# Loads, copies and small operations moved around the stage boundaries of a cross-attention and feed-forward kernel

## The reference

```python
x = x + xattn(layernorm(x), ctx)          # 4 batches of 512 rows, D = 1024, 64 context rows each
x = x + ffn(layernorm(x))
# xattn: q, k, v by Wq, Wk, Wv (16 heads of 96, 4 kv heads), softmax(q k / sqrt(96)) v, times Wo
# ffn:
rw = sum(top_k(z @ gate_w, 2))            # z = layernorm(x)
h = relu(z @ up_w) ** 2
y = h @ down_w + ((z @ fc1_w) @ expert_w * rw) @ fc2_w
x = x + ((y - mean(y)) * rsqrt(var(y) + 1e-5) * gamma + beta)
```

## Time and profile before

| | |
|---|---|
| median of three runs | 2058.83 us (2056.39 to 2061.26) |
| the profiled execution: its time, its span | 2057.5 us, 2055.7 us |
| TensorE busy, weight loads busy | 1988.4 us (97%), 1652.6 us (80%) |
| VectorE, ScalarE, GpSimd busy | 1206.9 (59%), 796.4 (39%), 798.2 us (39%) |
| mean granted TensorE clock | 0.985 |
| DMA moved | 357.83 MB, mean 174 GB/s |
| stage C, D, E on TensorE, from about | 917, 1237.8, 1654 us |

### The profile page before, as it was taken

How to read it: one execution, slowest core, us unless ns; L and a number is a source line. 1 busy time by engine, 2 the same in 40 slices (tenths; PEclk the granted TensorE clock), 3 DMA queues, 4 the chain that set the end, 5 groups by cost and what they waited for, 6 DMA issues and landing times. The chain is left out here.

```text
span 2055.7 us, 28449 instructions
## 1 busy us (share of the span) xinstructions
PE 1988.4 (97%) x9068; PEld 1652.6 (80%) x9068; DVE 1206.9 (59%) x1689; ACT 796.4 (39%) x1246; POOL 798.2 (39%) x593
## 2 busy tenths in 40 slices
PE   8999999999999999999899888999999999999996
PEld 7888888888888888887788676787778878888885
DVE  4222212178888888851334249987976754445698
ACT  5121111157777777761111115322634434333221
POOL 2533030137777777673112212111111155445442
PEclk9999999999999999999999999999999999999998
DMA  6754332536556666535577883657454576675755
GB/s 196 253 173 152 134 143 93 172 91 148 145 151 163 154 146 150 144 105 154 180 199 218 237 217 116 215 180 199 165 175 162 192 242 200 218 230 161 243 176 170
DMA packets 352573, 357.83 MB, mean 174 GB/s; under 512 B 148064, under 2 KB 246368, under 8 KB 351584
## 3 DMA queue, kind: packets, MB, share of 16 engines
q1 hardware_dynamic: 269856, 301.46, 47.2%
q10 hardware_dynamic: 82624, 55.19, 11.0%
HBM read 231.51 MB, written 124.80 MB: 173 GB/s over the span
## 5 line engine op out<-in xcount | busy, mean ns | idle before, releaser
L139 PE MATMUL psum<-operands 128*128 128x512 f32 (+3 forms) x2728 | 1058.6, 388 | 48.6 <-POOL operands L1507 14.1
L140 PE MATMUL psum<-operands 128*128 128x512 f32 (+3 forms) x2728 | 1055.2, 387 | 0.0
L141 PE MATMUL psum<-operands 128*128 128x512 f32 (+3 forms) x2728 | 1052.2, 386 | 0.0
L139 PEld LDWEIGHTS psum<-operands 128*128 128x128 f32 (+1 forms) x2728 | 518.1, 190 | 148.0 <-issue 35.5
L141 PEld LDWEIGHTS psum<-operands 128*128 128x128 f32 (+1 forms) x2728 | 518.3, 190 | 101.1
L140 PEld LDWEIGHTS psum<-operands 128*128 128x128 f32 (+1 forms) x2728 | 519.0, 190 | 89.1
L2378 POOL TENSOR_TENSOR operands<-operands 128x640 fp32r<-128x640 f32 x112 | 198.0, 1781 | 204.4 <-ACT operands L2374 204.3
L1183 DVE TENSOR_REDUCE small<-psum 128x1 fp32r<-128x576 f32 x256 | 192.9, 754 | 90.0 <-PE psum L1009 89.9
L926 POOL TENSOR_TENSOR operands<-staging,operands 128x512 fp32r<-128x512 f32 x128 | 164.4, 1292 | 30.5 <-ACT operands L1103 21.7
L1877 POOL TENSOR_TENSOR operands<-plain,operands 128x1024 fp32r<-128x1024 f32 x17 | 50.0, 2940 | 305.7 <-ACT operands L1869 305.7
L2374 ACT ACTIVATE operands<-operands 128x640 fp32r<-128x640 f32 x112 | 80.8, 735 | 200.7 <-DMA operands<-h_operand_scratch 200.7
(11 more groups left out here) (148 smaller groups left out, 1807.5 us busy)
## 6 DMA issues: line engine op xcount, KB each, us to landing
h_operand_scratch<-staging SPq DMA_DIRECT2D x70, 512.0 KB, 3.1
operands<-h_operand_scratch SPq DMA_DIRECT2D x112, 320.0 KB, 4.3
plain<-in_down_w SPq DMA_DIRECT2D x29, 512.0 KB, 6.3
plain<-in_up_w SPq DMA_DIRECT2D x28, 512.0 KB, 5.8
operands<-recip_scratch SPq DMA_DIRECT2D x64, 192.0 KB, 4.2
o_scratch<-staging SPq DMA_DIRECT2D x64, 192.0 KB, 5.0
operands<-o_scratch SPq DMA_DIRECT2D x64, 192.0 KB, 4.5
operands<-q_hi_scratch ACTq DMA_DIRECT2D x14, 768.0 KB, 6.0
```

The source lines that it names most:

```text
L139: e.matmul(o, lh, rh, start=first, stop=False)
L140: e.matmul(o, lh, rl, start=False, stop=False)
L141: return e.matmul(o, ll, rh, start=False, stop=last)
```

## The change

- **SP in stage C**: unit 0 of tile n + 1 is loaded right behind the store of x1 of tile n - 1, units 1 and 2 behind the load of the x row, the stores of x1 + beta and the fold, and unit 3 behind D's first loads; before, all four stood behind all of these. Expert_w and the first fc2_w quarter are loaded one tile sooner, each further quarter too.
- **ScalarE at the end of C**: z_hi 1, w_hi 1, w_hi 5, z_hi 6 and z_hi 5 stand ahead of the last z_out of the tiles, w_hi 6 behind it.
- **The turned z of jobs 4 and 5** goes to the staging (`SF[:, 6 D: 10 D]`), not to the place where z_sum 6 is written; the wait for their stores moves from `z_sum` to `u_sums(0)`.
- **VectorE**: w_lo 5 behind z_lo 5 at D's start; in the second half z_sum 5 behind `u_sums`, z_sum 4 and z_lo 6 ahead of `h21`. ScalarE's z_hi 5 of the second half is one step earlier.
- **Stage E**: units 6 and 7 are loaded ahead of the next pass's weights; the three small norm operations run on ScalarE behind the root; the last tile's last operation and its store are made in two halves, one stored by SP and one by ScalarE.

```diff
 def z_turned(j):
-    to = (plain((4 if j < 4 else 36) * D, SLOT), plain((6 if j < 4 else 38) * D, SLOT))[j % 2] if j < Z_EARLY else SF[:, 2 * D:3 * D]
+    if j < 4:
+        to = (plain(4 * D, SLOT), plain(6 * D, SLOT))[j % 2]
+    elif j < Z_EARLY:
+        to = SF[:, (6 + 2 * (j % 2)) * D:(8 + 2 * (j % 2)) * D]
+    else:
+        to = SF[:, 2 * D:3 * D]
     return to.rearrange("p (t d) -> p t d", d=D)
...
     def tiles(b, t0):
-        if b == FB:
-            e.dma_start(ex_raw, expert_w).then_inc(f_xld, 16)
-        for r in range(2 * G):
-            e.wait_ge(*past(b_os[r], b * (H // (2 * G) * 16) + H // (2 * G) * 16))
-            e.sem_inc(idle, 1)
         for t in range(t0, ST):
             n = b * ST + t
-            for u in range(0 if n != 1 else 3, 4):
-                c_load_unit(e, b, t, u)
             e.wait_ge(*past(cc_x1, n))
...
             e.dma_start(x1_d[bass.ds(n * P - P, P), :], XR).then_inc(cc_st, 16)
+            if n == FB * ST - 1:
+                e.dma_start(ex_raw, expert_w).then_inc(f_xld, 16)
+                f_load(e, 0)
+            if b == FB and t + 1 < NQ:
+                f_load(e, t + 1)
+            if n < LAST_C:
+                next_units(n + 1, (0,))
             e.wait_ge(*past(cc_st, n * 16))
...
                 e.dma_start(xb_tiles(n)[0], beta.partition_broadcast(P)).then_inc(bet_l, 16)
-            if b == FB:
-                f_load(e, t)
-                if t:
-                    f_store(e, t - 1)
+            if b == FB and t:
+                f_store(e, t - 1)
             if b == FB + 1 and t == 0:
                 f_store(e, NQ - 1)
+            if n < LAST_C:
+                next_units(n + 1, (1, 2))
             d_first_loads(e, n)
+            if n < LAST_C:
+                next_units(n + 1, (3,))
+    def next_units(n, units):
+        b, t = n // ST, n % ST
+        if t == 0 and 0 in units:
+            for r in range(2 * G):
+                e.wait_ge(*past(b_os[r], b * (H // (2 * G) * 16) + H // (2 * G) * 16))
+                e.sem_inc(idle, 1)
+        for u in units:
+            c_load_unit(e, b, t, u)
+    c_load_unit(e, 0, 1, 3)
     tiles(0, 1)
...
             f_evac(e, NQ - 1)
+        if n == LAST_C:
+            z_hi(e, 0, 1)
+            w_hi_op(e, 0, 1)
+            w_hi_op(e, 0, 5)
+            z_hi(e, 0, 6)
+            z_hi(e, 0, 5)
         if n >= 5 and n % 2 == 1:
             z_out(e, (n - 5) // 2)
-    z_hi(e, 0, 1)
-    w_hi_op(e, 0, 1)
-    w_hi_op(e, 0, 5)
+    w_hi_op(e, 0, 6)
...
     w_sum_op(e, 0, 6)
-    w_lo_op(e, 0, 5)
     w_sum_op(e, 0, 7)
...
     z_lo(e, 0, 5)
+    w_lo_op(e, 0, 5)
     tile(LAST_C)
...
         e.wait_ge(*past(z_tn, sum(Z_TURNS[:Z_EARLY])))
-    if q == 0 and p == 6:
-        z_stored(e, Z_EARLY - 2)
-        z_stored(e, Z_EARLY - 1)
     if p == 5:
...
-    z_hi(e, 0, 5)
-    z_hi(e, 0, 6)
-    w_hi_op(e, 0, 6)
     z_hi(e, 0, 2)
...
             z_hi(e, 1, 6)
+            z_hi(e, 1, 5)
         if end:
...
         if it == NF5 - 1:
-            z_hi(e, 1, 5)
             z_hi(e, 1, 7)
...
             e.wait_ge(*past(cc_st, 16 * B * ST))
+            z_stored(e, Z_EARLY - 2)
+            z_stored(e, Z_EARLY - 1)
         e.tensor_tensor(O22, product_bank(it, 6), O11, ALU.add).then_inc(d_sm, 1)
...
         prepare, end = it + 1 in FIRST_STEP, it == NIT - 1
+        if it == NF5:
+            z_sum(e, 1, 4)
+            z_lo(e, 1, 6)
         if it:
...
         if it == NF5:
-            z_sum(e, 1, 4)
-            z_lo(e, 1, 6)
             z_lo(e, 1, 2)
...
             w_sum_op(e, g + 1, 5)
+        u_sums(it)
         if it == NF5 - 1:
             z_sum(e, 1, 5)
-        u_sums(it)
         if it == 0:
...
 SUMS_A = [2, 1, 0, 1, 0, 0, 0]
-E_CHAIN, E_ROOT = 9, 4
+E_CHAIN, E_ROOT = 6, 5
...
         s, pr = g // NPR, g % NPR
+        if g == 0:
+            e_unit_load(e, NU)
+            e_unit_load(e, NU + 1)
         if s + 1 < NPASS:
...
         for n in (2 * g + NU, 2 * g + NU + 1):
-            if n < NUNITS:
+            if g and n < NUNITS:
                 e_unit_load(e, n)
...
             e_x1_load(e, norm_after(g - 2) + NX)
+    e_last_store(e, lo_cols, NT_E)
...
+def e_last_store(e, cs, done):
+    y, row = ln_tile(NT_E - 1)
+    e.wait_ge(*past(e_post, done))
+    e.dma_start(out_r[row * P:(row + 1) * P, cs], y[:, cs]).then_inc(e_st, 16)
 def e_act(e):
...
     def root(i):
+        def link(ins, n):
+            ins.then_inc(e_sq, 1)
+            e.wait_ge(*past(e_sq, 4 * i + n))
         e.wait_ge(*past(e_ch, E_CHAIN * i + E_ROOT))
-        e.activation(rt[:, 0:1], rec[:, 0:1], ACT.Sqrt).then_inc(e_sq, 1)
+        e.wait_ge(*past(e_post, i))
+        link(e.activation(rt[:, 0:1], rec[:, 0:1], ACT.Sqrt), 1)
+        link(e.activation(nt1[:, 0:1], rt[:, 0:1], ACT.Square), 2)
+        link(e.activation(nt1[:, 0:1], nt1[:, 0:1], ACT.Copy, bias=1.5, scale=rec[:, 1:2]), 3)
+        link(e.activation(rstd[:, 0:1], nt1[:, 0:1], ACT.Copy, scale=rt[:, 0:1]), 4)
...
     root(NT_E - 1)
-    out_store(NT_E - 1)
-    e.wait_ge(*past(e_st, 16 * NT_E))
+    e_last_store(e, hi_cols, NT_E + 1)
+    e.wait_ge(*past(e_st, 16 * NT_E + 16))
...
         link(e.scalar_tensor_tensor(y, y, mv[:, 0, 0:1], gam, ALU.subtract, ALU.mult))
-        e.wait_ge(*past(e_sq, i + 1))
-        link(e.scalar_tensor_tensor(nt1[:, 0:1], rt[:, 0:1], rt[:, 0:1], rec[:, 1:2], ALU.mult, ALU.mult))
-        link(e.tensor_scalar(nt1[:, 0:1], nt1[:, 0:1], 1.5, None, ALU.add))
-        link(e.tensor_tensor(rstd[:, 0:1], rt[:, 0:1], nt1[:, 0:1], ALU.mult))
+        e.wait_ge(*past(e_sq, 4 * i + 4))
         e.wait_ge(*past(e_xl[i % NX], 16 * (i // NX) + 16))
-        e.scalar_tensor_tensor(y, y, rstd[:, 0:1], x1b[i % NX], ALU.mult, ALU.add).then_inc(e_post, 1)
+        for cs in (lo_cols, hi_cols) if i == NT_E - 1 else (slice(0, D),):
+            e.scalar_tensor_tensor(y[:, cs], y[:, cs], rstd[:, 0:1], x1b[i % NX][:, cs], ALU.mult, ALU.add).then_inc(e_post, 1)
         assert n[0] == E_CHAIN
```

4 lines of the change are left out of this document (2 added, 2 removed).

## The result

| | before | after |
|---|---|---|
| median of 4 runs, us | 2057.61 (2055.42 to 2061.26) | 2031.56 (2027.82 to 2034.14) |
| ratio, 95% interval | | 0.987 (0.985 to 0.989) |
| profiled execution, us | 2057.5 | 2033.2 |
| its span, us, and granted clock | 2055.7, 0.985 | 2031.3, 0.991 |
| last matmul to end of span, us | 17.7 | 7.4 |

The kernel is 26 us faster, 34 were forecast. The profiled execution shows 24.4 of them by its span.

A forecast was written before the change was run, and what follows sets the result against it. TensorE, busy 97%, was taken as the bound: only its idle time, the slow clock after it or work behind its last matmul counts. Gains 7 + 12 + 3 + 2 + 10 = 34 us gave 2024, range 2011 to 2034.

The forecast's parts named there:

- Fold loads: Before the first fold product: loads one tile ahead shrink the 8.97 us pause to 2.2; gain 7 us, bounds 5 and 9.
- from there its own list is unchanged ... 10.2 us: VectorE, from the root to the first fold product's start: same operations, still 10.2 us, so the product starts near 1003.5.
- the 2.2 us: Pause expected to remain before the first fold product: start near 1003.5, TensorE free at 1001.3.
- Unit loads and D's start: Tile 13 to D's sixth product: tiles 13, 15 and D start without pause; gain 12 us, bounds 6 and 24.
- the pause of 6.96 reappears as 6.2 one tile later: Tile 13's pause moves to tile 14, whose first unit's copy stands behind z_out's eight DMAs on ScalarE; 6.2 us.
- z_out now stands ... to 1234.0 at 13.2 us: ScalarE at D's start: z_out issues from 1220.8 for 13.2 us, then w_hi 6; third product waits 1.4 us.
- the slower case: Rival, chance 0.03: z_outs of tiles 11, 13, 15 each issue 13 us longer, time 2063 or more.
- the second rival: At D's start z_out takes 21 us for 13 with d_next_loads beside it, holding w_hi 6; time 2032, chance 0.10.
- Last turned z in staging: D's start: z_sum 6's 15.19 us wait for z_out's DMAs goes; D starts at 1224.0, not 1237.78.
- D's second half: u_sums moved ahead removes the 2.15 us pause, splits come late next; gain 3 us, bounds 0 and 7.8.
- E's first loads: Stage E: units 6 and 7 loaded ahead of weights, pause of 3.85 shrinks to 1.9; gain 2 us, bounds 0 and 5.6.
- Small operations and halves: End of last pass: norm operations on ScalarE, last tile halved, VectorE catches up; gain 10 us, bounds 6 and 10.5.

The follow-up runs named there:

- 184.2 above: The four loads of fc2's quarters put back to their late places against the changed kernel, early unit loads and early expert weights kept; 2063.7 us (one run), tile 3 to 11 184.2.
- the experiment: Orders of D's second half and the loads of E's first two units put back as before, against the changed kernel; 2029.4 us (one run).

## Why the prediction was right and wrong

The range held the time, faster was right, and most of the signs came: no pause before tiles 13 and 15 and at D's start, z_out's eight issues and the unit's copy before tile 14, VectorE idle in the last pass, 7.4 us at the end for 7.6. Two did not come: there is no pause left before the first fold product, where about 2 us were expected, and inside D's first chunk stands one pause of 9.90 us, not one or two of 1 to 3. The value of 2024 was 7.6 too low. By its steps:

- **Fold loads**, forecast 7, measured 10.8. The mechanism held. Two terms were mis-sized by 2 us each. Counted from the sum of tile 3 (985.0 before, 987.8 after), VectorE went on 6.2 us later, where the forecast has 8.3. And "from there its own list is unchanged ... 10.2 us" took 8.2 to the end of the last split: the length of that list held 2.0 us of operations that ran beside GpSimd before and alone after. So TensorE found its operands ready and neither the 2.2 us nor the slow clock stayed. The term left out that the early units need these loads (184.2 above).
- **Unit loads and D's start**, forecast 12, measured 2.6: the step that failed. Of its parts, "the pause of 6.96 reappears as 6.2 one tile later" was right in kind and in size (5.7 to 8.0 in six kernels, 10.2 and 11.2 in two, the first of them the kernel after). "z_out now stands ... to 1234.0 at 13.2 us", with 1.4 us to wait for w_hi 6, was wrong: it took 22.7, in the other kernels of this order 23.0 to 24.1, and TensorE waited 9.90 and then ran at 0.59. I had taken the length of z_out from the earlier trace rows as a property of z_out, where it is one of what is ahead of it; and I wrote against the slower case that no new traffic came near z_out, which the unit loads' new place brought exactly there. It was the second rival, "D's start held by w_hi 6 behind z_out" (21 us, time 2032, chance 0.10), that described what happened. That its time fits to 1 us is luck in part: fold and tile 1 differ too.
- **Last turned z in staging.** VectorE's wait of 15.19 us is gone, D began right behind tile 15's last matmul, without a pause. It was not undone by itself, since z_out would then have to stand ahead of the copies again; but with the units late 8.6 us were gained here over before (130.6 to 122.0), and of the changes only this and the orders on ScalarE and VectorE are left there.
- **D's second half**, forecast 3, measured 0.1 (1 by the experiment). The sign given for its low bound came: the splits of the new half, wanted sooner, took the place of the sums, 3.05 + 1.14 + 1.64 us.
- **E's first loads**, forecast 2, measured 3.3 in the pair, 2.4 in the experiment (1 to 3 by the scatter); the pause stands one tile later, as the forecast had it, at 2.79 us for 1.9.
- **Small operations and halves**, forecast 10, measured 10.3. The Trainium skill, page "ScalarE: Activation LUTs" (section "Rules for kernel authors"), sends such arithmetic to VectorE; here four of them at 0.20 to 0.29 us run beside one wide operation of 1.27, and the trace goes against the rule by 9.8 us, because VectorE was the last engine and ScalarE idle.
- **z_out's cost of issue.** The rule of the Trainium skill, page "DMA: Bandwidth & Descriptors" (section "Issuing engines are not separate DMA queues"), that the issuing time is usually small beside the transfer, holds here for a pair with nothing of its own in flight (1.3 us) and not for eight (10 to 24 us; in the kernel after 22.7 of the 25.2 us until the last of them landed).

What stays open: what sets the limit of two to three such DMAs, and whether it counts pieces or DMAs. The profile names only "issue".

## What to carry to other kernels

An engine that computes and also issues DMAs is blocked for as long as the issue takes, and here that length depended on what another engine had issued ahead of it and beside it more than on the DMAs themselves. When loads are moved forward, look for the first long row of issues on every engine that they now pass, and size it as unknown; put such DMAs out in pairs between the copies that others wait for, each when the pair before it has moved. Test parts of a change in pairs: here early units cost 6 or over 20 us or gained 12, by what stood beside them. And a stretch of a list that ran beside another engine is not a length of that list: two operations of VectorE took 3.71 us beside GpSimd and 1.70 alone.

## What the hardware showed that I had not expected

The same eight DMAs (128 KB each, in pieces of 128 bytes) took ScalarE 9.9 to 24.1 us to issue, depending on which loads SyncE had issued shortly before. With w_hi 6 ahead of z_out the first two go out in 1.3 us even then, the next three take 9.15, 6.83 and 3.43 us, and the last three 0.7 each. In all 14 traces ScalarE was never further ahead than 2899 pieces, 2.8 of these DMAs, and an issue that took under 0.76 us began with at most 2346 pieces unmoved. SyncE is held the same way: four took 12.0 and 10.2 us there in D's first step, and 2.7 later on.
